# Attention on one core: three score banks with maxima per head, three key banks with exponentials per head, and rows turned 13 images later

## The reference

```
attn = softmax(q k^T / 4)            # first pass: all 256 keys of the image
out  = attn v, heads joined, @ W^T + bias + t
t    = t + softmax(mask(q k^T / 4)) v, joined, @ Wo^T     # second pass, q, k, v from rows = ln(t)
gate = ln(t) @ Wg^T                                       # logits of the first mixture
```

## Time and profile before

| | us |
|---|---|
| median of three runs | 867.62 (866.97 to 867.73) |
| profiled execution | 864.95, span 863.2 |
| TensorE products / VectorE / ScalarE / GpSimd busy | 688.5 / 612.1 / 418.2 / 424.5 |
| reductions of line 782, 128 of them | 139.6 |
| TensorE's products of line 586 waiting for the maximum | 11.6 |
| the mask products of line 623 waiting for it | 10.8 |

### The profile page before, as it was taken

One profiled execution on the slowest core, in us unless ns is written; L12 is line 12 of the kernel. 1 busy time (PEld: TensorE's weight loads), 2 busy tenths in 40 slices (PEclk: granted clock), 3 DMA queues, 4 the chain that ended last, 5 costly groups with the idle time before them and its releaser, 6 DMA issues. The chain is left out here.

```text
span 863.2 us, 21250 instructions
## 1 busy us (share of the span) xinstructions
PE 688.5 (80%) x7173; PEld 521.9 (60%) x7173; DVE 612.1 (71%) x1648; ACT 418.2 (48%) x829; POOL 424.5 (49%) x560
## 2 busy tenths in 40 slices
PE   0658899999999999997746998784988787359994
PEld 0234566666666666665545887762666666349993
DVE  3765578788877777876598888767567776647764
ACT  0355466665655544553264666520766666134442
POOL 0236102222227888879405777702555787724551
PEclk9979999999999999999566999985999999669995
DMA  6740000000000000000001222413400000122216
GB/s 175 225 164 1 2 3 2 3 3 3 2 3 4 3 15 15 21 16 21 25 1 34 53 53 54 47 7 106 119 2 2 14 17 17 53 68 72 65 46 195
DMA packets 42316, 37.39 MB, mean 43 GB/s; under 512 B 8947, under 2 KB 34536, under 8 KB 42212
## 3 DMA queue, kind: packets, MB, share of 16 engines
q1 hardware_dynamic: 35300, 24.55, 10.0%
q0 software_dynamic: 4800, 9.40, 4.8%
q10 hardware_dynamic: 2112, 2.10, 0.8%
HBM read 26.76 MB, written 9.46 MB: 42 GB/s over the span
## 5 line engine op out<-in xcount | busy, mean ns | idle before, releaser
L782 DVE TENSOR_REDUCE attend_negmax<-ps 128x4 f32<-128x1024 f32 (+1 forms) x128 | 139.6, 1090 | 82.9 <-PE ps L586 82.2
L729 ACT ACTIVATE attend_prob<-ps 128x1024 f32<-128x1024 f32 (+1 forms) x128 | 110.7, 865 | 137.2 <-PE ps L596 137.2
L586 PE MATMUL ps<-attend_key,attend_query 32*128 32x256 f32 (+2 forms) x1024 | 124.8, 360 | 12.8 <-DVE attend_negmax L782 11.6
L596 PE MATMUL ps<-attend_query,attend_key 32*128 32x256 f32 (+2 forms) x1024 | 124.6, 359 | 1.1 <-ACT attend_prob L729 1.0
L586 PEld LDWEIGHTS ps<-attend_key,attend_query 32*128 32x128 f32 x1024 | 79.6, 184 | 53.5 <-issue 45.7
L1777 POOL DMA_INDIRECT sums_xs<-table,sums_source x79 | 76.6, 969 | 56.8 <-DVE sums_source L1710 33.0
L596 PEld LDWEIGHTS ps<-attend_query,attend_key 32*128 32x128 f32 x1024 | 88.3, 184 | 2.3 <-issue 2.2
L1495 PE MATMUL ps<-sums_xT,sums_own 128*128 128x128 f32 x632 | 84.0, 279 | 0.0
L1495 PEld LDWEIGHTS ps<-sums_xT,sums_own 128*128 128x128 f32 x632 | 78.3, 195 | 0.0
L522 POOL TENSOR_SCALAR attend_rstd<-attend_spread 128x2 f32<-128x2 f32 x32 | 7.5, 234 | 130.7 <-DVE attend_spread L837 130.7
L1838 ACT ACTIVATE sums_hidden<-ps 128x512 f32<-128x512 f32 x79 | 47.2, 597 | 34.2 <-PE ps L1495 34.1
(11 more groups left out here) (346 smaller groups left out, 1616.7 us busy)
## 6 DMA issues: line engine op xcount, KB each, us to landing
attend_query<-attend_negmaxT SPq DMA_DIRECT2D x512, 0.5 KB
w<-in_L_ffn_w SPq DMA_DIRECT2D x1, 4096.0 KB, 27.9
expert_xs<-slots SPq DMA_DIRECT2D x39, 64.5 KB, 1.9
x<-in_x ACTq DMA_DIRECT2D x4, 512.0 KB, 8.3
table<-rows SPq DMA_DIRECT2D x16, 128.0 KB
experts<-in_L_ffn_W SPq DMA_DIRECT2D x1, 2048.0 KB, 8.7
experts<-in_L_ffn_W SPq DMA_DIRECT2D x4, 512.0 KB, 9.6
rows<-outputs SPq DMA_DIRECT2D x8, 256.0 KB, 4.9
```

Source lines behind the costliest of these rows:

```text
L586: return nc.tensor.matmul(ps[:, SCORE + i, at:at + width], query[rows, n % 3, odd, a * 128:(a + 1) * 128], key[rows, n % 3, odd, from_:fro ...
L596: return nc.tensor.matmul(ps[:, KEY_SCORE + i, at:at + width], key[rows, n % 3, odd, b * 128:(b + 1) * 128], query[rows, n % 3, odd, from_ ...
L729: nc.scalar.activation(of_pair(t // 4, t % 4)[:, :, 0:wide], ps[:, KEY_SCORE:KEY_SCORE + 2, 0:wide], ACT.Exp).then_inc(prob_ready, 1)
L782: last = nc.vector.tensor_reduce(out=negmax[:, s % 2, 0:4].rearrange("p (a r) -> p r a", a=2), in_=ps[:, SCORE:SCORE + 2, 0:2 * width].rea ...
```

## The change

- **Three score banks.** `SCORE` gets three banks, which the heads take in turn (`score_bank`). The maximum is taken head by head, two reductions over 128x512 (128x384 in the second pass) for one, each with its own count of `scored`. The wait of TensorE before slot s is for the first head of slot s - 1.
- **Maxima without the transpose.** `turn_max` goes. SP copies straight out of `negmax`, in which a query is a partition: in the first pass two copies a slot, in the second four. So that the first-pass copy is one row of pairs, `by_query` takes every second query column as its weights there (`own`). The reduction of slot s waits for the copies of slot s - 4 (so far the transpose did).
- **Three key banks in images 0 to 11.** `key_bank` takes the `TURN` bank as the third, and the exponential is made per head, two for one. From image 12 it is as before, on two banks.
- **Rows turned later.** For the first pass, `turn_rows` and `take_rows` become `turn_in` and `take_in`, 13 images behind instead of five (`BEHIND`), so in slots of images 13 to 28. The rows of the second pass stay five behind.
- **One bank for rows and logits.** `MISC` goes; logits share `TURN` with both kinds of rows, guarded by `free_turn`. `gate_logits` moves from the third slot to the first, `take_logits` from the fourth to the second.

```diff
-    SCORE, KEY_SCORE, PROJECT, HEADS, TURN, MISC = 0, 2, 4, 5, 6, 7
+    SCORE, KEY_SCORE, PROJECT, HEADS, TURN = 0, 3, 5, 6, 7
+    KEY_BANKS = (KEY_SCORE, KEY_SCORE + 1, TURN)
+    BY_HEAD = 4 * (IMAGES - 4)
+    BEHIND = 13
...
-        negmax = sb("negmax", [128, 2, 32])
-        negmaxT = sb("negmaxT", [128, 4, 32])
+        negmax = sb("negmax", [128, 4, 2, 2])
...
+        def key_bank(t, i):
+
+            return KEY_BANKS[(2 * t + i) % 3] if t < BY_HEAD else KEY_SCORE + i
+
+        def exponentials(t):
+
+            return 2 * min(t, BY_HEAD) + max(t - BY_HEAD, 0)
+
+        def score_bank(s, i):
+
+            return SCORE + (2 * s + i) % 3
...
+        def placed(k):
+
+            return 32 * min(k, IMAGES) + 64 * max(k - IMAGES, 0)
...
-                    sp.wait_ge(max_turned, s + 1)
                     for i in range(2):
                         row = free_row(groups[i], odd)
+                        sp.wait_ge(max_ready, 2 * s + i + 1)
+                        if not windowed(n):
+                            sp.dma_start(query[row:row + 1, n % 3, odd, :], negmax[:, s % 4, i, :])\
+                                .then_inc(max_placed[s % 4], 16)
+                            continue
                         for a in range(2):
                             sp.dma_start(query[row:row + 1, n % 3, odd, a * 128:(a + 1) * 128],
-                                         negmaxT[2 * a + i::32, s % 4, :]).then_inc(max_placed[s % 4], 16)
+                                         negmax[:, s % 4, i, a:a + 1]).then_inc(max_placed[s % 4], 16)
...
                         if s >= 1 and not windowed(n):
-                            pe.wait_ge(max_ready, s)
+                            pe.wait_ge(max_ready, 2 * s - 1)
...
-                        return nc.tensor.matmul(ps[:, SCORE + i, at:at + width],
-                                                query[rows, n % 3, odd, a * 128:(a + 1) * 128],
+                        own = slice(a * 128, (a + 1) * 128) if windowed(n) else slice(a, N, 2)
+                        return nc.tensor.matmul(ps[:, score_bank(s, i), at:at + width],
+                                                query[rows, n % 3, odd, own],
...
-                        return nc.tensor.matmul(ps[:, KEY_SCORE + i, at:at + width],
+                        return nc.tensor.matmul(ps[:, key_bank(t, i), at:at + width],
...
-                        pe.wait_ge(max_placed[t % 4], 64 * (t // 4 + 1))
+                        pe.wait_ge(max_placed[t % 4], placed(t // 4 + 1))
                         if t >= 1:
-                            pe.wait_ge(prob_ready, t)
+                            pe.wait_ge(prob_ready, 2 * t - 1 if t < BY_HEAD else exponentials(t))
...
+                def free_turn(n):
+
+                    if n == IMAGES - 3:
+                        pe.wait_ge(prob_ready, exponentials(BY_HEAD))
+                    if n - 6 >= IMAGES:
+                        pe.wait_ge(rowsT_ready, min(n - 5 - IMAGES, IMAGES))
+                        pe.wait_ge(logits_taken, min(n - 5 - IMAGES, IMAGES))
+
+                def turn_in(k):
+                    pe.wait_ge(rows_ready, k + 1)
+                    if k >= 1:
+                        pe.wait_ge(in_ready, k)
+                    for a in range(2):
+                        mm = nc.tensor.transpose(ps[:, TURN, a * 128:(a + 1) * 128], rows[:, 2 * k + a, 0:C], ident)
+                    mm.then_inc(in_turned, 1)
...
                             project_out(n - 4)
+                        if runs(n - 6) and windowed(n - 6):
+                            gate_logits(n - 6)
...
-                        if runs(n - 6) and windowed(n - 6):
-                            gate_logits(n - 6)
-                        if runs(n - 5):
+                        if n >= BEHIND:
+                            free_turn(n)
+                        if 0 <= n - BEHIND < IMAGES:
+                            turn_in(n - BEHIND)
+                        if runs(n - 5) and windowed(n - 5):
                             turn_rows(n - 5)
...
+                    if t < BY_HEAD:
+                        for i in range(2):
+                            act.wait_ge(key_scored[i], t + 1)
+                            nc.scalar.activation(to[:, i], ps[:, key_bank(t, i), 0:wide], ACT.Exp)\
+                                .then_inc(prob_ready, 1)
...
+                def take_in(k):
+                    act.wait_ge(in_turned, k + 1)
+                    if k + BEHIND - 5 >= IMAGES:
+                        act.wait_ge(rows_turned, k + BEHIND - 4 - IMAGES)
+                    nc.scalar.activation(xf[:, k * N:(k + 1) * N], ps[:, TURN, 0:N], ACT.Copy).then_inc(in_ready, 1)
...
-                    dve.wait_ge(scored, 2 * s + 2)
-                    if s == 0:
-                        dve.wait_ge(zeros_set, 1)
+                    if s >= 4:
+                        dve.wait_ge(max_placed[s % 4], placed(s // 4))
                     width = 192 if windowed(s // 4) else 256
...
+                    for i in range(2):
+                        dve.wait_ge(scored[i], s + 1)
+                        nc.vector.tensor_reduce(out=negmax[:, s % 4, i, :],
+                                                in_=ps[:, score_bank(s, i), 0:2 * width].rearrange(
+                                                    "p (a n) -> p a n", a=2),
+                                                axis=AX.X, op=ALU.max, negate=True).then_inc(max_ready, 1)
...
+                        if runs(n - 6) and windowed(n - 6):
+                            take_logits(n - 6)
...
-                    if s < SLOTS:
-                        turn_max(s)
```

More of the change, by code:

```diff
@@ L415, in attend @@
         vaug_ready = sem("vaug_ready")
-        scored = sem("scored")
+        scored = [sem(f"scored{i}") for i in range(2)]
         max_ready = sem("max_ready")
-        max_turned = sem("max_turned")
         max_placed = [sem(f"max_placed{r}") for r in range(4)]
-        key_scored = sem("key_scored")
+        key_scored = [sem(f"key_scored{i}") for i in range(2)]
         prob_ready = sem("prob_ready")
@@ L437, in attend @@
         rowsT_ready = sem("rowsT_ready")
+        in_turned = sem("in_turned")
+        in_ready = sem("in_ready")
         logits_done = sem("logits_done")
@@ L508, in keep_window @@
                     k = t - 4 * IMAGES
-                    pool.wait_ge(prob_ready, t + 1)
+                    pool.wait_ge(prob_ready, exponentials(t + 1))
                     both = prob[:, t // 4 % 2, t % 4, 0:768].rearrange("p (h b n) -> p h b n", h=2, b=2)
@@ L633, in weigh @@
                     else:
-                        pe.wait_ge(prob_ready, 4 * n + 2 * g + 2)
+                        pe.wait_ge(prob_ready, exponentials(4 * n + 2 * g + 2))
                     for b, from_, width, at in BLOCKS[windowed(n)]:
@@ L664, in gate_logits @@
                     k = n - IMAGES
-                    pe.wait_ge(rowsT_ready, n + 1)
+                    pe.wait_ge(rowsT_ready, k + 1)
+                    pe.wait_ge(in_ready, min(n + 6 - BEHIND, IMAGES))
                     if k >= 1:
@@ L728, in exponential @@
                     wide = WIDE[windowed(t // 4)]
-                    nc.scalar.activation(of_pair(t // 4, t % 4)[:, :, 0:wide], ps[:, KEY_SCORE:KEY_SCORE + 2, 0:wide],
-                                         ACT.Exp).then_inc(prob_ready, 1)
-                def take_rows(n):
-                    act.wait_ge(rows_turned, n + 1)
-                    if not windowed(n):
-                        out = xf[:, n * N:(n + 1) * N]
-                    else:
-                        if n >= IMAGES + 2:
-                            act.wait_ge(logits_done, n - IMAGES - 1)
-                        out = rowsT[:, n % 2, :]
-                    nc.scalar.activation(out, ps[:, TURN, N:2 * N], ACT.Copy).then_inc(rowsT_ready, 1)
+                    to = of_pair(t // 4, t % 4)[:, :, 0:wide]
+                    if t < BY_HEAD:
[3 more added lines that the diff above has]
+                                .then_inc(prob_ready, 1)
+                    else:
+                        for i in range(2):
+                            act.wait_ge(key_scored[i], t + 1)
+                        nc.scalar.activation(to, ps[:, KEY_SCORE:KEY_SCORE + 2, 0:wide], ACT.Exp).then_inc(prob_ready, 1)
+                def take_in(k):
[3 more added lines that the diff above has]
+                    nc.scalar.activation(xf[:, k * N:(k + 1) * N], ps[:, TURN, 0:N], ACT.Copy).then_inc(in_ready, 1)
+                def take_rows(n):
+                    k = n - IMAGES
+                    act.wait_ge(rows_turned, k + 1)
+                    if k >= 2:
+                        act.wait_ge(logits_done, k - 1)
+                    nc.scalar.activation(rowsT[:, k % 2, :], ps[:, TURN, N:2 * N], ACT.Copy).then_inc(rowsT_ready, 1)
                 take_query(0)
@@ L753, in _ @@
                     if j == 3:
-                        if runs(n - 5):
```

(7 more changed lines are left out.)

36 lines of the change are left out of this document (11 added, 25 removed).

## The result

The changed kernel takes 874.75 us (median of 4 runs, 873.48 to 877.76); the kernel before, on the same chip, 867.3. The ratio of the means is 1.0099 [1.0063, 1.0135]: slower by about 1%, where 849 was forecast. The profiled execution took 875.5, its span is 873.8.

The account below looks back on a forecast made before the run. TensorE's order of work was taken as the bound, with 23.2 us idle. Gains of 9.1 us in the first pass and 9.3 in the second made 18.4, so 867.6 became 849 us; range 843 to 862, the forecast's own 844 to 855.

Parts of the forecast that it names:

- the price of the copies: SP's issues of maxima copies: 0.53 us each at most, 9.0 us per second-pass image, just below TensorE's sum.
- SP as the bound: Rival: SP or its queue binds the second pass, 10.2 us an image at 0.6 an issue; 858.5 us, chance 0.14.
- The rival with slow packets: Small packets slow second-pass copies; from 0.6 us a copy that pass loses, beyond 0.64 the kernel is slower; chance 0.13.
- Nothing comes of it: Rival: waits of the same length fill the idle pieces; 867.6 us, bounds 866 to 869, chance 0.07.
- the strided weights: First-pass `by_query` loads of every second column: forecast to cost nothing; as rival 0.37 us a load, 858 us, chance 0.09.
- The reduction and the three score banks: Reductions per head, 0.65 us first pass, 0.54 second; rings shrink to 2.00 and 1.92, so TensorE binds.
- The first pass: Images 0 to 15 of `attend`: 9.1 us gained, images 2 to 12 taking 9.4 us for 10.09.
- The ScalarE wait of 0.2 an image: First pass: a new TensorE wait of about 0.2 us an image at the next image's key-major products, behind the exponential.
- matters once an image: First pass: the exponential holds up TensorE only after the third slot, where ScalarE first takes query and keys.
- the score ring: First pass: products fill the score banks, VectorE empties them, TensorE refills; 2.57 us a slot before, 2.00 forecast.
- Row turns and logits: Later row turns save 0.31 us in images 5 to 12, return in 13 to 28; earlier logits cost nothing.
- The landing: Maxima copies have 11 us until the key-major products five slots on; 0.65 + 2.1 + even 5.9 fits.

Follow-up runs that it names:

- the runs with ScalarE: Changed kernel with one of a second-pass slot's four maxima copies issued by ScalarE instead of SP: 852.39 us, ratio 0.9850.
- with small copies: Changed kernel with one head's first-pass copy cut into 16, 16, 32 and 64 partitions, or into 4, 4, 8 and 112: 941.87 and 939.83 us.
- with rows of 128 bytes: Changed kernel with second-pass maxima transposed by VectorE again, so each copy is four rows of 128 bytes: 841.85 us, ratio 0.9725.
- eight buffers: Changed kernel with eight tiles for the maxima in place of four: 877.1 us, ratio 1.0124.

## Why the prediction was wrong

**The step that failed** is the price of the copies: "An issue of 128 four-byte rows took 0.43, so I leave it at 0.53 at most." Behind one another they took 0.601 by the median and 0.642 on average, the long issues counted in, and 0.043 lie between two. An image of the second pass then costs SP 16 x 0.685 + 0.59 for the row write = 11.55 us, in place of 9.0, and images 20 to 30 take 11.55 on average. The row chosen was the cheap one of its line, and it follows on one large copy, not on others of small pieces. Issues directly behind it, of 32 KB each in rows of 512 and 256 bytes, were to be seen in the same view of the kernel before:

```profile
L2255 SPq DMA_DIRECT2D w_wq_r<-in_L_conv_wq_r x1: 433/433/433, 1.7 to 1.7; - x1
L2255 SPq DMA_DIRECT2D w_wv_r<-in_L_conv_wv_r x1: 608/608/608, 2.2 to 2.2; - x1
L2255 SPq DMA_DIRECT2D w_w_up<-in_L_conv_w_up x1: 576/576/576, 2.9 to 2.9; - x1
```

A queue that was forecast to be busy 9.0 of 9.03 us had to be priced by issues that follow others of their kind, and by their upper end.

**The rivals.** SP as the bound had 0.14 and its place, but it was priced as the second pass's gain lost, 858.5. Its own figure, 10.2 an image, was already above the 9.79 of before: 16 x 10.2 = 163 us where the second pass took 153.4, so this rival should have been priced at about 868, no gain at all. The rival with slow packets had the right form of sum: beyond 0.6 us a copy the second pass loses. 256 x (0.685 - 0.6) = 21.8; measured 22.1. That they meet is partly luck. The sum leaves out 16 row writes, some 10 us; and the pass, read by its reductions, ends at 406.6, while SP's last copy goes out at 413.4. Its break-even of 0.64 a copy lay just below what came. It named the packets as the cause, which the runs with ScalarE and with small copies refute. Both rivals were one mechanism, SP's issues. "Nothing comes of it" can be dropped, since the first pass gained, and so can the strided weights: line 609's loads take 191 ns by the row below (103 to 230 us), against 184.

```profile
L838 DVE TENSOR_REDUCE attend_negmax<-ps 128x2 f32<-128x512 f32 x110 | 70.9, 686 | 21.5 <-PE ps L609 21.5
...
L609 PEld LDWEIGHTS ps<-attend_key,attend_query 32*128 32x128 f32 x432 | 38.3, 191 | 17.6 <-issue 11.1 <-DVE attend_negmax L838 4.1
```

**The reduction and the three score banks**: right. A half takes 0.69 in the first pass (0.65 forecast) and 0.55 in the second (0.54), and TensorE binds in the first pass, and in the second with rows of 128 bytes.

**The first pass**: 12.9 us where 9.1 was forecast. The ScalarE wait of 0.2 an image did not come: images take 9.17, and TensorE's own sum without the wait was 2.46 + 2.31 + 2.17 + 2.24 = 9.18. That is 2.2 of the 3.8 us more. The rest is in the first images, 0 to 3, which gained 0.5, 1.2, 1.3 and 1.3 us where 0.35 each (0 and 1) and 0.7 each (2 and 3) were forecast; images 13 to 15 together gained less, 0.3 for 0.7. The working behind it, that the exponential "matters once an image", was wrong: with two key banks it is a ring in every slot, as long as the score ring was. The gain came only because the change removes both.

**Row turns and logits**: no cost shows, for the returned transposes less than the 0.31 an image of the forecast: in the kernel with rows of 128 bytes images 22 to 28, which have them, average 9.10 us, images 29 and 30 without them 9.13. With rows of 128 bytes the second pass's images 17 to 20 average 8.76 (8.7 forecast), 21 takes 8.9 (9.0), 22 to 28 average 9.10 (9.34). That pass gains 9.0 us (153.36 to 144.33), forecast 9.3: TensorE's sum was right, and only SP stood in front of it.

**The landing**: 2.0 us by the median, of the 11 us that it had, and the queue's packets took 14.1% of 16 engines in 281.10 to 406.70 us. Neither binds.

```profile
attend_query<-attend_negmax SPq DMA_DIRECT2D x256, 0.5 KB, 2.0
```

```profile
q1 hardware_dynamic: 27567, 1.31, 14.1%
```

The Trainium skill, "Perfetto Trace Analysis", section "What "DMA-bound" means", lists the issuing engine's track, solid with issues, as a bound of its own beside the transfer engines, and recommends large descriptors for it. This case is that one (two pauses of 0.34 us between 231.7 and 414.0), and rows of 128 bytes did cure it; but not by their number, since four small pieces cost what 128 do.

## What to carry to other kernels

Price a queue's issues as a rate: take the price from issues that follow directly on one another, of the same kind of copy, and where the sum comes close to the loop it feeds, take the upper end. A rival that makes an engine the bound is priced by that engine's time per pass of the loop, not by the gain that goes. And where two resources are emptied in rings of the same length (score banks by VectorE, key banks by ScalarE), freeing one shows nothing; look for the second before the first is costed.

## What was not expected of the hardware

- What an issue costs hangs on the copy before it. Directly behind a copy of small pieces an issue of such a copy takes 0.59 to 0.60 us (244 of the 256 of line 500, median 0.601), and a row write 0.59, where it takes 0.44 behind rows of 128 bytes. The other 12 of line 500 take 0.469 to 0.477: two after a pause, ten directly behind the row write. ScalarE's, each after a pause, take 0.476. In the first pass SP issues the second copy of a slot 0.13 after the first is done; it takes 0.517, so that it still ends 0.645 after the first. Four rows of 128 bytes take 0.492 behind another or not. Why stays open.

```profile
L800 ACTq DMA_DIRECT2D attend_query<-attend_negmax x64: 476/477/559, 231.3 to 384.1; - x64
```

- Among the copies of small pieces some issues take 0.9 to 1.9 us, 20 of the 256 in the changed kernel's second pass, or about one an image. The kernel before had none above 0.674 among its 512 copies, the one with rows of 128 bytes again had two, 0.77 and 0.87. None of the 20 waits for a reduction: ten are the second copy of a head, which the program lets wait for nothing, and for the other ten the reduction had ended 0.2 to 7.3 us before SP was free. What holds them up stays open. They make up the difference between the median of 0.601 and the mean of 0.642.
- TensorE's clock falls to 1.2 GHz three times in the changed kernel's second pass, 13.6 us in all. Two windows (in the first TensorE is idle for 2.35 us on end, waiting for a reduction):

```profile
351.00:354.40 3.40, 1.05 (x27) 0.69 (x24) 1.62 (x7) 0.31 (x1) 1.68 (x3) 1.00 0.11 1
354.40:357.80 3.40, 3.40 (x20) 2.42 (x12) 2.36 (x9) 1.79 (x4) 1.46 (x2) 0.52 0.11 1
```

`project` takes 2.08 us there in place of 1.13. Half of 13.6, 6.8 us, is the most that this alone can add to the 22.1; with eight buffers the clock was low for only 6.8 us of the second pass, which still took 173.1. With rows of 128 bytes it stays at 2.4 GHz through both passes.
